# Layer 2's low halves by accumulating DMAs from GpSimd instead of VectorE subtractions, in a two-layer convolution kernel

## The reference

```python
x = x + _L0_conv_ref(_gn(x), L0_conv_weight, L0_conv_bias)   # 9x9, weights are Gaussians made from (sx, sy, angle), zero padding, bias
x = x + _L1_conv_ref(_gn(x), L1_conv_weight)                 # 5x5, circular convolution by FFT over a reflect-padded image
```

## Time and profile before

| | |
|---|---|
| median of three runs | 244.52 us (244.44 to 244.59) |
| span of the profiled execution | 242.7 us |
| TensorE busy (matmuls) | 232.7 us, 1447 matmuls |
| VectorE busy | 212.9 us |
| ScalarE busy | 155.7 us |
| GpSimd busy | 4.4 us |

### The profile page before, as it was taken

One profiled execution on the slowest core, in us unless ns is written; L12 is line 12 of the kernel. 1 busy time (PEld: TensorE's weight loads), 2 busy tenths in 40 slices (PEclk: granted clock), 3 DMA queues, 4 the chain that ended last, 5 costly groups with the idle time before them and its releaser, 6 DMA issues.

```text
span 242.7 us, 4170 instructions
## 1 busy us (share of the span) xinstructions
PE 232.7 (96%) x1447; PEld 144.7 (60%) x1447; DVE 212.9 (88%) x463; ACT 155.7 (64%) x333; POOL 4.4 (2%) x12
## 2 busy tenths in 40 slices
PE   5699999899999999999999999999999999999995
PEld 5467666555566665555666665556666665655554
DVE  4989999699999999999989998999997359978943
ACT  5888898999399567999537592537358003569210
POOL 1000000050000000000000000000000000000000
DMA  6980022220015000003412000063020001521123
GB/s 207 379 332 4 6 72 54 69 64 0 3 41 167 7 1 0 0 3 101 136 75 97 0 4 0 12 185 115 1 100 0 0 0 46 163 101 55 48 97 97
DMA packets 8709, 17.24 MB, mean 71 GB/s; under 512 B 3312, under 2 KB 5616, under 8 KB 8688
## 3 DMA queue, kind: packets, MB, share of 16 engines
q1 hardware_dynamic: 7712, 16.64, 20.9%
q10 hardware_dynamic: 976, 0.34, 0.5%
HBM read 5.57 MB, written 4.72 MB: 42 GB/s over the span
## 4 chain that ended last, share of the span: by engine, by line
PE 71%; DVE 16%; ACT 6%; issue 3%; DMA 2%; ACTq 0%; DVEq 0%
PE banks L1425 34%; PE banks L1442 33%; DVE X L766 4%; PE banks L1389 3%; ACT junk L1059 3%; DVE lo L733 2%; DMA tab<-in_tables 2%; DVE whl L563 2%; PE banks L1501 1%; DVE work L558 1%; DVE s L703 1%; DVE partU L719 1%; ACT hi L1115 1%; PE banks L1375 1%; DVE s L706 1%
## 5 line engine op out<-in xcount | busy, mean ns | idle before, releaser
L1425 PE MATMUL banks<-hi,whl 128*128 128x360 f16 (+4 forms) x576 | 99.1, 320 | 1.4 <-ACT hi L1115 1.2
L1425 PEld LDWEIGHTS banks<-hi,whl 128*128 128x128 f16 x576 | 56.0, 99 | 35.7 <-issue 1.7
L1425 PE MATMUL banks<-lo,whl 128*128 128x376 f16 (+4 forms) x288 | 51.6, 320 | 0.5 <-DVE lo L733 0.5
L1059 ACT ACTIVATE junk<-X 128x576 bf16<-128x576 f32 x58 | 39.5, 681 | 2.1 <-DVE X L766 0.5
L1425 PEld LDWEIGHTS banks<-lo,whl 128*128 128x128 f16 x288 | 28.0, 98 | 17.9 <-DVE lo L733 1.1
L1442 PE MATMUL banks<-lo,wh 128*128 128x384 f16 (+1 forms) x165 | 31.8, 323 | 0.0
L1442 PE MATMUL banks<-hi,wh 128*128 128x384 f16 (+1 forms) x165 | 31.8, 323 | 0.0
L1442 PE MATMUL banks<-hi,wl 128*128 128x384 f16 (+1 forms) x165 | 31.8, 323 | 0.0
L1115 ACT CAST hi<-work 128x416 f16<-128x416 f32 x32 | 16.6, 536 | 19.9 <-PE banks L1442 14.1
L1115 ACT CAST hi<-s 128x384 f16<-128x384 f32 x32 | 15.3, 508 | 17.9 <-DVE s L700 12.2
L1105 ACT ACTIVATE work<-work,gof,gsc 128x26 f32<-128x26 f32 (+1 forms) x48 | 23.3, 576 | 3.6 <-DVE gof L644 3.6
(11 more groups left out here) (138 smaller groups left out, 231.7 us busy)
## 6 DMA issues: line engine op xcount, KB each, us to landing
X<-in_x SPq DMA_DIRECT2D x8, 576.0 KB, 9.6
out<-X SPq DMA_DIRECT2D x7, 576.0 KB, 3.0
work<-X SPq DMA_DIRECT2D x8, 432.0 KB, 3.8
whl<-work SPq DMA_DIRECT2D x24, 64.0 KB, 2.0
work<-X SPq DMA_DIRECT2D x8, 144.0 KB, 3.6
stage<-in_w SPq DMA_DIRECT2D x1, 640.0 KB, 7.6
work<-X SPq DMA_DIRECT2D x32, 12.0 KB, 2.3
out<-X SPq DMA_DIRECT2D x1, 384.0 KB, 2.6
```

The costliest lines, as they stand in the source:

```text
L1059: nc.scalar.activation(waste, image(n, m), function, accum_out=sums[c][:, col:col + 1]).then_inc(sums_done[c], 1)
L1425: ins = nc.tensor.matmul(dst[:, :, o0:o1], w[1][:, i, t * P:(t + 1) * P], src[:, :, o0 + dx:o1 + dx], start=(first and part == 0 and t == ...
```

## The change

Layer 2's low halves are no longer subtracted on VectorE. ScalarE, right after each layer 2 cast to hi, writes the negated stream, rounded to float16, into the lo buffer (`nc.scalar.mul(..., -1.0)` of the same float32 stream, so it equals minus hi). GpSimd then issues one DMA per stream that reads the float32 stream from `s32_2`, casts it and adds it to lo. The 32 subtractions leave VectorE's list, 32 activations enter ScalarE's, 32 DMAs enter GpSimd's, and the waits on `lo_done[2]` become waits on these DMAs' landing, one semaphore for each stream position k.

```diff
@@ streams2
-                wait(dve, hi_done[2], 4 * n)
-                wait(dve, lo_done[2], 4 * n)
+                wait(dve, negative_done, 4 * n)
+                for k in range(4):
+                    wait(dve, lo2_landed[k], 16 * n)
@@ second_quad (and every other low_halves(2, ...) of the lists)
                 streams2(0)
-                low_halves(2, 0, range(4))
                 small_stats(1, 2)
@@ last_steps
                 rows2(n + 1)
                 streams2(n + 2)
-                low_halves(2, n + 2, range(2))
                 end2(n + 1, 2)
-                low_halves(2, n + 2, range(2, 4))
                 end2(n + 1, 3)
                 streams2(n + 3)
@@ high_half
                 nc.scalar.copy(hi[c][:, i, :], src).then_inc(hi_done[c], 1)
+                if c == 2:
+                    nc.scalar.mul(lo[2][:, i, :], src, -1.0).then_inc(negative_done, 1)
@@ gpsimd
             normalise_last(1)
+            for n in range(NP):
+                for k, i in enumerate(S2):
+                    pool.wait_ge(negative_done, 4 * n + k + 1)
+                    pool.dma_start(lo[2][:, i, :], s32_2[:, i, :], accum_op=ALU.add).then_inc(lo2_landed[k], 16)
@@ conv2
                     if part == 1:
-                        pe.wait_ge(lo_done[2], 4 * n + k + 1)
+                        pe.wait_ge(lo2_landed[k], 16 * (n + 1))
```

More of the change, by code:

```diff
@@ L265, in build @@
         lo_done = {c: sem(f"lo{c}_done") for c in (1, 2)}
+        negative_done = sem("negative_done")
+        lo2_landed = [sem(f"lo2_landed{k}") for k in range(4)]
         conv_mm = {c: sem(f"conv{c}_mm") for c in (1, 2)}
@@ L929, in second_quad @@
                 streams2(1)
-                low_halves(2, 1, range(2))
                 middle1(1, 2)
                 middle2(0)
-                low_halves(2, 1, range(2, 4))
                 streams1_near(2)
@@ L959, in third_quad @@
                 streams2(2)
-                low_halves(2, 2, range(4))
                 middle1(2, 1)
@@ L964, in third_quad @@
                 streams1_near(3)
-                low_halves(2, 3, range(2))
                 middle1(2, 2)
                 rows1(2, 2)
-                low_halves(2, 3, range(2, 4))
                 low_halves(1, 3, range(2))
@@ L990, in fourth_quad @@
                 streams2(4)
-                low_halves(2, 4, range(4))
                 end1(3, 2)
@@ L1005, in last_steps @@
                 rows2(n)
-                low_halves(2, n + 1, range(2))
                 end2(n, 2)
-                low_halves(2, n + 1, range(2, 4))
                 end2(n, 3)
@@ L1020, in last_steps @@
                 rows2(n + 2)
-                low_halves(2, n + 3, range(2))
                 end2(n + 2, 2)
-                low_halves(2, n + 3, range(2, 4))
                 end2(n + 2, 3)
```

## The result

The changed kernel takes 248.41 us (median of four runs, 248.24 to 248.62) against 244.49 us (244.44 to 244.59) for the kernel before, measured beside it: 3.9 us slower, ratio 1.0154 with a 95% interval of 1.0126 to 1.0183. The forecast was 251.5 us, with a range of 247.0 to 262.0 us.

What follows compares the result with a forecast made beforehand. TensorE was taken to bound the kernel from 92 us on. Waits at set 0 (2.9), set 1 (0.7), the statistics (0.4) and set 6 (3.0) sum to 2L - 2.0 = 7.0 us; 244.52 + 7.0 = 251.5 us, range 247.0 to 262.0.

Steps and rivals of the forecast that it cites:

- rival A: GpSimd's added DMA is as cheap as a plain copy of its float32 bytes: landing 2.7 us, 247.9 us; chance 0.15.
- The bound: From the first layer 2 set (92 us) on, TensorE bounds: any time it waits is added to the end.
- L = 4.5 us: Time from a negation's end until TensorE may use lo; taken as 4.5 us, low end 1.8, high end 7.6.
- The set 0 term: TensorE's wait for the first low half of layer 2's set 0: L - 1.6, forecast at 2.9 us.
- the set 6 term: TensorE's wait for the first low half of layer 2's set 6: L - 1.5, forecast at 3.0 us.
- Set 1, 0.7 us "whatever L is": Further wait at set 1's first low half after set 0's wait is taken off: 0.7 us, if its streams are in time.
- The statistics, 0.4 us: TensorE's matmuls on the sums after set 4: a negation ahead of the last read makes them wait 0.4 us.
- Set 7, 0.75 us to spare: Set 7's first low half, its streams awaiting set 6's fourth landing: ready at 233.0 us, wanted at 233.75, no wait.
- VectorE's 17 us, costed at nothing: Removing 32 subtractions, 17.4 us of VectorE, is worth nothing to the end, being covered by TensorE's own work.
- B: DMAs are slow or queue on GpSimd, issues over 1.0 us or VectorE in the way: 254 us and up; chance 0.24.
- C: Not slower: with L under 1.5 us, lo of sets 0 and 6 arrives in time; about 244.5 us; chance 0.04.
- D: TensorE's clock falls in a wait, costing 3.4 us for two waits at 1.7 us each: 254.9 us; chance 0.04.

Runs made afterwards that it cites:

- the mixed version: Against the changed kernel: VectorE makes six of the 32 low halves, DMAs the other 26, and the store of pair 5 is held; 244.52 us, ratio 0.9996.

## Why the prediction was right, and where it was off

- **The number.** 248.41 us is inside the range, but not in the likeliest interval (249 to 254 us, 0.53). It lies in rival A's, 246.5 to 249 us, which had been given 0.15, and 3.9 us came where 7.0 were forecast. The direction and most of the places held, the size did not; the wide range is what makes the number right.
- **The bound.** Right. After 92 us each us that TensorE loses is at the end: 4.06 us in the profiled execution, whose span grew by 4.1 us.
- **L = 4.5 us.** The step that was mis-sized. It measured 3.31 us at set 0 and 3.14 us at set 6. The nearest row was taken by bytes (416 KB moved, 3.8 us), with 0.54 us for the queue on top. But a plain GpSimd copy of 104 KB lands in 1.9 us, issue included, and adding and casting bring the first of a set to 2.8 to 3.0 us. With 3.2 us in it, the prediction's 2L - 2.0 gives 4.4 us, 248.9 us, against 248.41 measured. The set 0 term, L - 1.6, gives 1.7 us (measured 1.66); the set 6 term, L - 1.5, gives 1.6 us (1.63).
- **Set 1, 0.7 us "whatever L is".** Wrong by its working, not by its form. A cast and its negation take 0.88 us and not 1.0, and the cast expected at 101.1 us started at 100.57; 0.03 us were lost. Its real weight showed when set 0's wait was taken away: 2.17 us.
- **The statistics, 0.4 us.** Right, 0.40 us, of which 0.10 is the matmuls' own longer time, which the working did not have; present in each run that keeps the negation of set 5's third stream, absent in the mixed version.
- **Set 7, 0.75 us to spare.** Wrong: 0.34 us lost although L was shorter. The fourth landing of set 6 was put at L like the others and took 5.6 us. The prediction spoke of traffic beside the transfers but gave it no price.
- **VectorE's 17 us, costed at nothing.** Right as to a gain: with low halves left out there is none. Wrong as to cover: with VectorE adding, ScalarE's negations cost 3.1 us, 2.1 of them at a place in layer 1 that I had not looked at. The prediction should have named VectorE's relief as what hides them.
- **Rivals.** A (a landing of 2.7 us, 247.9 us) came nearer in time than the forecast, though the landing was 3.5 us in the median, and its reason, that cast and addition cost nothing, is wrong: they cost 0.9 us a landing at sets 0 and 6. The Trainium skill's fit for a GpSimd DMA (page "DMA: Bandwidth & Descriptors", section on the anatomy of a SWDGE DMA), which gave an estimate of 2.5 us for 213,000 bytes, lies under the 3.0 us that the first one took here. For 104 KB the same fit gives an estimate of 2.2 us, where the plain copy took 1.9. The measurements decide. B fell: an issue takes 0.86 us in the median, at most 1.08 us for those of set 0, and they start 0.9 us apart, which is the pitch of ScalarE's negations. VectorE doesn't stand in GpSimd's way here: two issues from 105.84 us took 1.74 us, 0.87 us each, beside a VectorE that works on two inputs throughout, and four from 221.69 us took 3.52 us, 0.88 us each, with VectorE idle from 222.9 us. This agrees with what the Trainium skill infers for two-input operations (page "SBUF — State Buffer", section "Who interferes with whom"). C fell, and D too: the clock stayed at 1.00 in the profiled execution, and the only matmuls that were slower behind a wait by more than 0.01 us are the statistics' two, by 0.11 us together.

The rows behind this, from the timelines of GpSimd and VectorE in the changed kernel:

```profile
105.84 1.74 POOL L1352 DMA_DIRECT2D lo<-work  x2 [2.26 <-ACT lo L1107]
...
221.69 3.52 POOL L1352 DMA_DIRECT2D lo<-work  x4 [7.66 <-ACT lo L1107]
```
```profile
105.70 0.96 DVE L684 SCALAR_TENSOR_TENSOR partU<-P,partU 128x768 f32<-128x768 f32 x1
106.79 1.03 DVE L696 TENSOR_TENSOR s<-partU 128x384 f32<-128x384 f32 x2
...
230.09 0.59 DVE L743 TENSOR_TENSOR work<-work 128x416 f32<-128x416 f32 x1 [7.16 <-DMA lo<-work]
```

Open: why set 0's issues took up to 1.08 us, why cast and addition together cost more than their sum beside other transfers, and what besides the store holds up the later transfers of set 6. The path from the negations to quad 2's waits was read from one trace and not tested by itself.

## What to carry to other kernels

When an operation moves to a DMA, what counts is not its throughput but how long after its source is ready the consumer asks, at each place; here sets 0, 1 and 6 ask within 2 us and are exposed, while sets 2 to 5 have more than the 3.3 us and pay nothing. Take the places away one by one only with care: a wait at one gives slack to the next, so price each deadline as if the earlier waits were gone. And before calling freed time on an engine worthless, ask which added work elsewhere it covers.

## What the runs showed of the hardware that was not expected

An accumulating, casting DMA of 104 KB from GpSimd landed 2.8 to 3.5 us after its issue where only others like it ran (sets 0 and 1), and up to 6.0 us beside a store of 576 KB. Without cast and addition the same shape took 1.9 us in the median. Counted at the places where TensorE waits, the addition costs 0.64 us and the cast 0.23 us, a price in latency that a copy's row doesn't show. GpSimd's queue is held 0.86 us by an issue with addition and 0.53 us by one without, so half of the addition's price is paid there.
